# 13 of 25 one-hot tiles kept in DRAM by the first pass and loaded back in the message and attention passes

## The reference

```python
x = _layernorm(x + _L0_gnn_ref(x, edge_index, ...), axis=-1)   # one segment_sum of x[src]
x = _layernorm(x + _L1_gnn_ref(x, edge_index, ...), axis=-1)   # one segment_sum of x[src]
x = _layernorm(x + _L2_gnn_ref(x, edge_index, edge_attr_16, ...), axis=-1)
#   three times: m = relu(cat(h[src], h[dst], edge) @ W1 + b1) @ W2 + b2; segment_sum(m, dst); GRU cell
x = _layernorm(x + _L3_gnn_ref(x, edge_index, ...), axis=-1)
#   twice: e = leaky_relu(a_s[src] + a_d[dst]); softmax over dst; segment_sum(alpha * h[src], dst)
```

## Time and profile before

| | us |
|---|---|
| median of 3 runs (3472.44 to 3480.63) | 3476.05 |
| the profiled execution, as timed | 3476.43 |
| its span in the profile | 3474.6 |

### The profile page before, as it was taken

How to read it: one execution, slowest core, us unless ns; L and a number is a source line. 1 busy time by engine, 2 the same in 40 slices (tenths; PEclk the granted TensorE clock), 3 DMA queues, 4 the chain that set the end, 5 groups by cost and what they waited for, 6 DMA issues and landing times.

```text
span 3474.6 us, 70518 instructions
## 1 busy us (share of the span) xinstructions
PE 2573.1 (74%) x26212; PEld 2297.6 (66%) x26212; DVE 2873.3 (83%) x8394; ACT 1286.9 (37%) x2442; POOL 2375.1 (68%) x2279
## 2 busy tenths in 40 slices
PE   7898559993887775678775777774798983699861
PEld 6778349993476675477665576774388883588861
DVE  7987489984479999579998689997789996989987
ACT  0000110100465663465663556652424442033342
POOL 7777637777377775677774777764477775677762
PEclk9999669996898897688887788987699996699985
DMA  4435314432134443234444244443023222122321
GB/s 112 131 111 119 97 36 152 152 115 79 31 105 128 131 135 114 74 104 130 133 131 119 63 112 133 136 122 105 16 59 77 75 71 59 36 72 74 74 66 29
DMA packets 259981, 332.01 MB, mean 96 GB/s; under 512 B 108777, under 2 KB 117811, under 8 KB 259474
## 3 DMA queue, kind: packets, MB, share of 16 engines
q1 hardware_dynamic: 179230, 241.48, 21.7%
q0 software_dynamic: 72576, 73.37, 11.7%
q10 hardware_dynamic: 7924, 14.13, 1.1%
HBM read 193.94 MB, written 134.83 MB: 95 GB/s over the span
## 4 chain that ended last, share of the span: by engine, by line
DVE 48%; PE 21%; issue 13%; POOL 13%; ACT 3%; DMA 2%; DVEq 1%; SPq 0%; POOLq 0%; ACTq 0%
PE ps L1432 16%; DVE big L888 13%; POOL ringG L594 11%; DVE ringG L919 8%; DVE ringG L1026 5%; DVE ringQ L919 5%; DVE ringG L969 3%; PE ps L1402 3%; DVE ringG L963 2%; POOL gN L594 2%; ACT ringG L722 1%; DVE ringG L912 1%; DVE big L904 1%; PE ps L1411 1%; DVE running_max L1010 1%
## 5 line engine op out<-in xcount | busy, mean ns | idle before, releaser
L594 POOL DMA_INDIRECT ringG<-tab,src_i x1677 | 1754.5, 1046 | 597.9 <-issue 469.1
L1432 PE MATMUL ps<-big 128*128 128x192 bf16 (+1 forms) x23270 | 2118.1, 252 | 4.6 <-DVE big L888 3.0
L1432 PEld LDWEIGHTS ps<-big 128*128 128x128 bf16 x23270 | 2006.8, 100 | 33.6 <-issue 17.1
L919 DVE SCALAR_TENSOR_TENSOR ringG<-ringG,same 128x64 f32<-128x64 f32 x2075 | 581.8, 280 | 98.6 <-DMA ringG<-tab,src_i 40.8
L888 DVE TENSOR_SCALAR big<-big,node_f 128x1280 bf16<-128x1280 int16 (+1 forms) x1030 | 582.9, 584 | 27.1 <-PE ps L1432 26.6
L888 DVE TENSOR_SCALAR big<-src_hot_b,node_f 128x1280 bf16<-128x1280 int16 (+1 forms) x1011 | 572.8, 585 | 25.4 <-PE ps L1432 25.0
L1432 PE MATMUL ps<-opener,big 128*128 128x448 bf16 (+1 forms) x455 | 211.9, 493 | 419.5 <-ACT big L678 335.3
L1432 PEld LDWEIGHTS ps<-opener,big 128*128 128x128 bf16 x455 | 55.0, 121 | 518.4 <-ACT big L678 401.2
L594 POOL DMA_INDIRECT ringG<-in_x,src_i x286 | 301.1, 1053 | 87.6 <-issue 84.4
L919 DVE SCALAR_TENSOR_TENSOR ringQ<-ringQ,same 128x64 f32<-128x64 f32 x1245 | 347.2, 279 | 3.0
L678 ACT COPY big<-ps 128x384 f32<-128x384 f32 (+3 forms) x429 | 164.6, 478 | 401.4 <-PE ps L1432 401.3
(11 more groups left out here) (233 smaller groups left out, 1863.5 us busy)
## 6 DMA issues: line engine op xcount, KB each, us to landing
sums<-ringG SPq DMA_DIRECT2D x260, 256.0 KB
ringE<-ef_mix SPq DMA_DIRECT2D x156, 256.0 KB, 3.3
ringQ<-q_at_start SPq DMA_DIRECT2D x156, 256.0 KB, 3.2
sums_w<-ringG SPq DMA_DIRECT2D x104, 264.0 KB
ringG<-tab,src_i POOLq DMA_INDIRECT x1677
q_at_start<-gN ACTq DMA_DIRECT2D x52, 256.0 KB
ef_mix<-ringE SPq DMA_DIRECT2D x64, 208.0 KB
big<-hot_src SPq DMA_DIRECT2D x27, 320.0 KB
```

The source lines that it names most:

```text
L594: return pool.indirect_dma_start(out=out_ap, out_offset=None, in_=table, in_offset=bass.IndirectOffsetOnAxis(ap=index, axis=0))
L919: return v.scalar_tensor_tensor(now, before if u == 0 else source[:, (u - 1) * D:u * D], same[:, c:c + 1], now, ALU.mult, ALU.add)
L1432: mm = pe.matmul(ps[:, b, 0:256 + n] if wide else ps[:, b, to:to + n], hot[t][:, u * P:(u + 1) * P], opener[:, 0:256 + n] if wide else spl ...
```

## The change

The first pass still makes all 25 tiles of every unit, and now SyncE also stores 13 of them (4, 3, 3 and 3 of the pieces, the first ones of each) in new DRAM tensors `kept0` to `kept3`. The message and attention passes load these 13 tiles into `big` instead of making them. `FED` names how many; `mine(q)` begins behind them. ScalarE makes 4 tiles of a unit in the message passes, where it made 6; none in attention, as before. VectorE is left with 8 in message (19 before) and 12 in attention (25 before). For the tiles to be the same, the attention passes take 10 hot columns of 32 instead of 11, so GpSimd gathers 22 columns a trip there instead of 21. Pass 1 keeps 11 hot columns and makes its tiles as before. In the first pass VectorE waits (`hot_kept`) until a piece of the unit before is stored before it overwrites it. TensorE waits for `hot_fed` beside `hot_ready`.

```diff
-        return TILES[q][:len(TILES[q]) - self.lent[q]]
+        return TILES[q][self.fed[q]:len(TILES[q]) - self.lent[q]]
...
-FIRST_HOT, GIN_HOT, MSG_HOT, GAT_HOT = (3, 2, 3, 2), (3, 3, 3, 2), (3, 2, 3, 2), (3, 3, 3, 2)
-LENT = (2, 2, 1, 1)
-PASSES = ([Pass(0, FIRST_HOT), Pass(1, GIN_HOT)] + [Pass(2 + l, MSG_HOT, lent=LENT) for l in range(NLAYER)]
-          + [Pass(5 + l, GAT_HOT, WG) for l in range(2)])
+KEPT_HOT, GIN_HOT = (3, 2, 3, 2), (3, 3, 3, 2)
+FED, LENT = (4, 3, 3, 3), (1, 1, 1, 1)
+FIRST_FED = 2
+PASSES = ([Pass(0, KEPT_HOT), Pass(1, GIN_HOT)] + [Pass(2 + l, KEPT_HOT, D, FED, LENT) for l in range(NLAYER)]
+          + [Pass(5 + l, KEPT_HOT, WG, FED) for l in range(2)])
...
+        kept = [dram(f"kept{q}", (TRIPS * P, FED[q] * sum(KEPT_HOT) * P), BF16) for q in range(len(TILES))]
...
+        def fed_tiles(q):
+            size = sum(KEPT_HOT) * P
+            return big[:, 0:5 * NP].bitcast(BF16)[:, TILES[q].start * size:(TILES[q].start + FED[q]) * size]
...
+                    if k >= FIRST_FED and i + 2 < TRIPS:
+                        feed_piece(k, i + 2, j)
                     store_sums(k, g)
+                    if k == 0 and i + 2 < TRIPS:
+                        keep_piece(i + 2, j)
+
+            def keep_piece(i, q):
+                sp.wait_ge(hot_ready, len(TILES) * i + q + 1)
+                sp.dma_start(kept[q][i * P:(i + 1) * P], fed_tiles(q)).then_inc(hot_kept[q], 16)
+
+            def feed_piece(k, i, q):
+                way, m = PASSES[k], k * TRIPS + i
+                if i == 0:
+                    sp.wait_ge(bank_done, BANKS_BEFORE[k])
+                elif q < len(TILES) - 1:
+                    sp.wait_ge(hot_used, (len(TILES) - 1) * (m - 1) + q + 1)
+                else:
+                    sp.wait_ge(bank_done, BANKS_BEFORE[k] + i * way.banks)
+                sp.dma_start(fed_tiles(q), kept[q][i * P:(i + 1) * P]).then_inc(hot_fed[q], 16)
...
             for dst, s in weight_loads:
                 sp.dma_start(dst, s).then_inc(weights_in, 16)
+            for i in range(2):
+                for q in range(len(TILES)):
+                    keep_piece(i, q)
...
+                feed_unit(2 + l, 0)
                 sp.wait_ge(q_scattered, 16 * NT * (l + 1))
                 for g in range(QRING):
                     load_starts(l, g)
+                feed_unit(2 + l, 1)
...
+                feed_unit(5 + l, 0)
                 sp.wait_ge(ad_scattered, 16 * NT * (l + 1))
                 sp.dma_start(ad_e[:].rearrange("p l o -> p (l o)"), ad_g).then_inc(ad_in, 16)
+                feed_unit(5 + l, 1)
...
             act.wait_ge(weights_in, 16 * len(weight_loads))
+            for q in range(len(TILES)):
+                act.wait_ge(hot_kept[q], 16 * TRIPS)
...
                     v.wait_ge(src_hot_in[m % 2], 16 * (m // 2 + 1))
+                if k == 0 and i:
+                    v.wait_ge(hot_kept[q], 16 * i)
...
                 pe.wait_ge(hot_ready, at(len(TILES), k * TRIPS * len(TILES) + q + 1))
+                if way.fed[q]:
+                    pe.wait_ge(hot_fed[q], at(16, (k - FIRST_FED) * TRIPS * 16 + 16))
```

More of the change, by code:

```diff
@@ L82, with __init__ @@
 class Pass:
-    def __init__(self, k, hot, width=D, lent=(0, 0, 0, 0)):
-        self.k, self.hot, self.width, self.u, self.lent = k, hot, width, sum(hot), lent
+    def __init__(self, k, hot, width=D, fed=(0, 0, 0, 0), lent=(0, 0, 0, 0)):
+        self.k, self.hot, self.width, self.u, self.fed, self.lent = k, hot, width, sum(hot), fed, lent
         self.banks = -(-self.u // 2)
     def mine(self, q):
-        return TILES[q][:len(TILES[q]) - self.lent[q]]
+        return TILES[q][self.fed[q]:len(TILES[q]) - self.lent[q]]
     def theirs(self, q):
@@ L340, in build @@
         hot_ready, hot_used = sem("hot_ready"), sem("hot_used")
+        hot_kept, hot_fed = ([sem(f"{name}{q}") for q in range(len(TILES))] for name in ("hot_kept", "hot_fed"))
         gap_made, lent_ready = sem("gap_made"), sem("lent_ready")
@@ L500, in trip, with feed_unit @@
                             load_starts(l, g + QRING - 1)
+                    if k >= FIRST_FED and i + 2 < TRIPS:
+                        feed_piece(k, i + 2, j)
                     store_sums(k, g)
+                    if k == 0 and i + 2 < TRIPS:
[12 more added lines that the diff above has]
+                sp.dma_start(fed_tiles(q), kept[q][i * P:(i + 1) * P]).then_inc(hot_fed[q], 16)
+            def feed_unit(k, i):
+                for q in range(len(TILES)):
+                    feed_piece(k, i, q)
             def next_sources(k):
```

## The result

The changed kernel takes 3336.85 us (3333.68 to 3345.89), the kernel before 3477.98 us beside it: a ratio of 0.9604, interval 0.9592 to 0.9616. A second comparison (experiment 5) gave 3336.42 and 0.9600 (0.9584 to 0.9616). The forecast was 3337. The profiled execution has a span of 3334.4 us.

What follows compares the result with a forecast made beforehand. Message passes were taken as bound by a loop over VectorE, ScalarE and TensorE, with GpSimd close behind, and attention after the change by GpSimd. From 3476.4 us, -114 - 36 + 11 = -139 gave 3337 us; 8-in-10 range 3295 to 3405.

Steps and rivals of the forecast that it cites:

- The loop in the message passes: Message passes: VectorE, ScalarE and TensorE form a loop; fewer VectorE tiles shorten it, 38 us a pass, -114 us.
- The step that decided the sum: Message trips: only tiles removed in groups 0 to 2 shorten the loop, 3.4 us a trip; group 3 only lengthens its wait.
- The price of a gather: GpSimd, message and attention: fewer VectorE tiles bring a gather from 1.365 to 1.30 us, ends 1.25 and 1.365.
- one stretched gather: End of pass 0: a gather took 3.98 us behind a VectorE operation, read as VectorE, not DMA traffic, lengthening gathers.
- Rival (b): GpSimd: a gather stays at 1.365 us; message passes gain 93 us, attention loses 1; 3395 us, chance 0.11.
- (a): GpSimd is relieved fully, 1.25 us a gather; attention gains 64 us; about 3300 us, chance 0.14.
- The loads cost nothing: Message passes: loads of fed tiles, 4.26 MB a trip, hide under the 29 us trip; zero, within +-3 us a pass.
- (c): Message passes: DMA engines become the bound, trips up to 31 us, gain 46 us only; 3427 us, chance 0.09.
- (d): Message passes: TensorE waits for `hot_fed`, trips of 35.3 us at 240 GB/s; slower, about 3590 us, chance 0.05.
- Attention: Attention passes: bound by GpSimd's gathers, 379 us from first gather to end; gain 14 + 22, -36 us.
- First pass: Pass 0: stores behind the weight loads delay unit 2's sources, so VectorE and GpSimd start later; +11 us (5 to 18).
- the three terms: Whole kernel: message passes -114 us, attention passes -36 us, first pass +11 us; sum -139 us.

Runs made afterwards that it cites:

- experiment 5: The changed kernel once more, unedited, against the kernel before: 3336.42 us, ratio 0.9600.
- Experiment 2: The changed kernel with ScalarE copying the banks behind a message trip's third group instead of the fourth: 3311.75 us, ratio 0.9522 to the kernel before.
- experiment 3: The changed kernel with attention making all 25 tiles on VectorE again, still at 10 hot columns: 3361.51 us, ratio 0.9669 to the kernel before.
- the kernel with both edits: The changed kernel with unit 0's stores after 34 weight loads and banks copied behind the third message group: ratios 0.9882 and 0.9792 to the kernel before.
- experiments 1 to 3: The first: the changed kernel with unit 0's stores and unit 2's sources ahead of later weight loads, 3326.66 us; the others: Experiment 2 and experiment 3.

## Why the prediction was right

**The loop in the message passes.** The step that decided the sum was to count only tiles in groups 0 to 2, since those of group 3 fall into the wait for TensorE. It gave 38 us a pass; 35.5, 38.2 and 37.7 were measured. In pass 3 a trip went from 32.8 to 29.4 us, the 3.4 us forecast. L1011 waits 2.7 us a trip, forecast 2 to 3. Experiment 2 shows that it is this loop: with the banks copied a group earlier the wait goes and the passes shrink by 26 us without a tile less. That tiles of group 3 are worth nothing is borne out by these sums only; no run takes them out alone. Pass 2 is the exception: its 384.6 us are 286 gathers of 1.324 us and 6 us behind them, so there the price of a gather decided.

**The price of a gather.** Taken as 1.30 us, measured 1.31 to 1.32 in message and 1.28 to 1.29 in attention. That it hangs on VectorE was read from one stretched gather, which was not beside tiles; the conclusion was right, and experiment 3 now shows it for tiles. Rival (b), an unchanged 1.365, falls, and so does (a), the floor of 1.25.

**The loads cost nothing.** Forecast a DMA share of 0.85 to 0.95; it is 0.87 at 288 GB/s, and in the message stretch TensorE waits for no fed tile. It does at the start of passes 2, 5 and 6 (3.6, 14.5 and 13.8 us). In passes 5 and 6 it waited just as long for VectorE's tiles in the kernel before (15.7 and 15.3 us), and no stage grew by more than 2.3 us, so this costs next to nothing. Rivals (c) and (d) fall. Experiment 3 adds that this traffic does not make gathers dearer.

**Attention.** Gained 44 us for 36. The mechanism, a bound by gathers with VectorE waiting for them, is there, with 1.285 and 1.292 us a gather for 1.30 (4 and 2 us a pass); the last sum ends 6.4 and 6.7 us behind the last gather, forecast 7.3. What the forecast left out is how the gain came about: 26 us by the fed tiles, 18 by the 10 hot columns instead of 11, which it had counted as a cost of 17 us a pass (experiment 3).

**First pass.** The term was undersized: 14.8 us for 11. VectorE started unit 1 at 51.55 for 49.5, and unit 2 at 71.69 for 67. The first store was done 7.7 us after its issue and not 6 (the median of all 960 KB stores is 6.4), and the load of unit 2's sources, issued at 63.9 behind the last stores, took 7.8 us and not 5.5. The errors of the three terms (+2.6, -8.3, +3.8) nearly cancel, so the hit within 1 us is luck; within 10 us it is not.

```profile
kept<-big SPq DMA_DIRECT2D x39, 960.0 KB, 6.4
```

## What to carry to other kernels

When an engine is relieved, look for the loop it stands in and count only the work that lies inside the loop; then price the next engine, including what the relieved one does to it. A table that several passes need can be stored once and loaded again if the DMA engines have room, but its first stores and their waits belong ahead of other queued work, and the engine that opens the next round should be served as early as its inputs allow. A gain holds for the engine that sets the pace: where TensorE does, the kernel with both edits gained 1.2 and 2.1%, and the change without them 4.0% where it does not.

## What the runs showed of the hardware

A gather on GpSimd took 0.94 us with VectorE idle and 1.11 us beside bf16 compare operations in a row, whatever the DMA engines did (388 GB/s for the first, 48 and 409 for the second). In one stretch of attention it took 1.024 us on the mean with 25 of these operations a trip and 0.978 with 12. With tile stores running the DMA engines moved 388 GB/s over 14 us, above the 358 GB/s that the Trainium skill, "DMA: Bandwidth & Descriptors", section Specifications, gives as a core's HBM limit:

```profile
56.00:70.00 14.00, 14.00 (x146) 13.15 (x145) 9.79 (x21) 0.00 (x0) 8.18 (x8) 0.87 1.01 388
```

In some comparisons TensorE left about 1000 us of gaps between matmuls that wait for nothing the profile shows, the mean granted clock was 0.74 instead of 0.85, and the kernel before took 4910 to 5030 us instead of 3477. It is not a fixed property of a chip: chip 6 gave 3475 us for the kernel before in experiments 1 to 3 and 4910 us a quarter of an hour later. The gaps don't go with the DMA traffic either: on that chip they were 1017 us with 387 MB, 1082 with 664, 977 with 736 and 1096 with 766 MB. The cause is open.
